# Two cross attentions: a third score bank, maxima inside the query tile, and their transposition a head earlier

## The reference

```python
qh = q.reshape(B, h, dq, Lq)          # q is x: 16 x 128 x 256, h = 8 heads
kh = k.reshape(B, h, dq, Lk)          # k and v are the context
vh = v.reshape(B, h, dv, Lk)
qk = jnp.einsum('bhdq,bhdl->bhql', qh, kh) * scale
sm = jax.nn.softmax(qk, axis=-1)
ret = jnp.einsum('bhql,bhdl->bhdq', sm, vh)
return gamma * ret.reshape(B, Dv, Lq)
```

## Time and profile before

| what | value |
|---|---|
| median of three runs | 1437.89 us (1437.3 to 1447.53) |
| profiled execution | 1438.84 us, its span 1437.1 us |
| busy PE / PEld / DVE / ACT / POOL | 79 / 61 / 64 / 39 / 34% of the span |
| mean granted clock of TensorE | 0.904 of 2.4 GHz |
| DVE's maxima L388, ACT's exponentials L522 | 256 each, 686 and 597 ns |
| PE L296, L316, L318 | 512 each, printed mean 288, 280, 278 ns |

### The profile page before, as it was taken

The page is one execution under the profiler, slowest core; times in us unless marked ns, Lnnn a source line. Parts: engine busy times, 40 slices in busy tenths (PEclk is TensorE's granted clock), DMA queues, the critical chain, the costliest instruction groups (busy, mean ns, idle before and its releaser), DMA issues. The chain is left out here.

```text
span 1437.1 us, 31266 instructions
## 1 busy us (share of the span) xinstructions
PE 1139.4 (79%) x9497; PEld 883.2 (61%) x9568; DVE 915.0 (64%) x2406; ACT 558.5 (39%) x1306; POOL 492.5 (34%) x971
## 2 busy tenths in 40 slices
PE   4599998599964353345999999999999599986997
PEld 4466675366641122125998899898988366654665
DVE  3488995477758999982444444444445378765886
ACT  3245554266642121122323332333233166653553
POOL 5276886233322222221232233223223223322232
PEclk8889999699996667667999999999999699998999
DMA  7899995434424011001010010001001234431111
GB/s 152 176 183 225 189 168 114 115 115 122 128 75 93 23 33 33 25 22 63 12 38 23 29 33 25 22 29 37 22 19 34 83 116 128 124 89 49 55 51 41
DMA packets 145419, 111.84 MB, mean 78 GB/s; under 512 B 17872, under 2 KB 131840, under 8 KB 145344
## 3 DMA queue, kind: packets, MB, share of 16 engines
q1 hardware_dynamic: 132032, 100.01, 28.4%
q10 hardware_dynamic: 11344, 8.72, 2.2%
q0 software_dynamic: 1968, 2.16, 0.9%
HBM read 68.91 MB, written 31.52 MB: 70 GB/s over the span
## 5 line engine op out<-in xcount | busy, mean ns | idle before, releaser
L388 DVE TENSOR_REDUCE ca_nm<-ca_p_s 128x2 f32<-128x512 f32 x256 | 170.5, 686 | 79.4 <-PE ca_p_s L296 72.6
L522 ACT ACTIVATE ca_pt<-ca_p_e 128x512 f32<-128x512 f32 x256 | 152.0, 597 | 89.7 <-PE ca_p_e L318 88.2
L296 PE MATMUL ca_p_s<-ca_ks,ca_qs 96*128 96x256 bf16 x512 | 103.7, 288 | 41.5 <-DMA ca_ks<-k_stack 37.2
L316 PE MATMUL ca_p_e<-ca_qs,ca_ks 96*128 96x256 bf16 x512 | 130.3, 280 | 0.2
L318 PE MATMUL ca_p_e<-ca_mt,row_of 96*128 96x256 bf16 x512 | 129.0, 278 | 0.0
L2064 ACT ACTIVATE la_pq<-la_p_s,la_nm 128x128 f32<-128x128 f32 x256 | 73.2, 369 | 106.2 <-DVE la_nm L2104 106.2
L1897 PE MATMUL la_p_f<-la_qt,q_w 128*128 128x128 f32 x512 | 101.4, 280 | 12.5 <-ACT la_lt L2045 11.3
L1555 PE MATMUL mx_p_i<-identb,mx_qi 128*128 128x128 bf16 x128 | 19.4, 307 | 108.8 <-POOL mx_qi L1406 108.8
L1898 PE MATMUL la_p_f<-la_qt,q_w 128*128 128x128 f32 x512 | 99.0, 275 | 0.0
L296 PEld LDWEIGHTS ca_p_s<-ca_ks,ca_qs 96*128 96x128 bf16 x512 | 45.3, 101 | 69.2 <-DMA ca_ks<-k_stack 30.1
L1897 PEld LDWEIGHTS la_p_f<-la_qt,q_w 128*128 128x128 f32 x512 | 77.6, 192 | 16.3 <-ACT la_lt L2045 16.3
(11 more groups left out here) (282 smaller groups left out, 3009.6 us busy)
## 6 DMA issues: line engine op xcount, KB each, us to landing
sa_qks<-sa_qkp SPq DMA_DIRECT2D x96, 128.0 KB, 4.9
ca_qs<-q_stack SPq DMA_DIRECT2D x64, 192.0 KB, 2.9
ca_ks<-k_stack SPq DMA_DIRECT2D x64, 192.0 KB, 3.2
ca_ct<-in_ctx_t SPq DMA_DIRECT2D x32, 128.0 KB, 3.0
ca_xr<-x_state SPq DMA_DIRECT2D x32, 128.0 KB, 2.1
x_state<-ca_xn SPq DMA_DIRECT2D x32, 128.0 KB, 2.7
k_stack<-sa_cxp SPq DMA_DIRECT2D x16, 192.0 KB, 2.8
q_stack<-sa_parts SPq DMA_DIRECT2D x16, 192.0 KB, 2.6
```

Of the source, the lines that this page charges most:

```text
L296: last = pe.matmul(p_s[h % 2][:, qc, :], QS[u][:, h, 128 * qc:128 * qc + 128], KS[u][:, h, :], start=True, stop=True)
L316: pe.matmul(p_e[h % 2][:, kc, :], KS[u][:, h, 128 * kc:128 * kc + 128], QS[u][:, h, :], start=True, stop=False)
L388: dve.tensor_reduce(NM[u][:, h, :], p_s[h % 2][:, :, :], AX.X, ALU.max, negate=True).then_inc(max_done, 1)
L522: act.activation(PT[h // 4][:, h % 4, :, :], p_e[h % 2][:, :, :], ACT.Exp, scale=SCALE).then_inc(exp_done, 1)
```

## The change

- The maxima's rows go into the query tile itself. QS and KS get 128 partitions: 96 hold the stacks, and 32 more hold the transposed parts of the maxima (QS, written by `copy_max`, four times over, once for each head of the group) and a constant that selects a head's rows (KS, from `picks`). *Shifted* then needs two matmuls of 128 rows instead of four; `MT` goes, and the transposed maxima land on partitions 96 to 127.
- `set_picks` makes `picks` on POOL in the self attention, behind step 13; three copies on DVE put it into the three KS buffers at the start of each cross attention.
- Three banks for scores instead of two: scores of a head wait for the maxima three heads back. `p_r` moves into the bank of `p_t`, and `turn_out` takes over the wait that `turn_back` had.
- QS and KS have three buffers. One load brings all eight heads (384 KB), as soon as the image before the last one has been shifted.
- `turn_max` and `copy_max` stand one head earlier.
- All pairs of images are written out; no loop is left in this stage.

```diff
-        QS = [sb(f"qs{u}", [STACK, H, D], BF16) for u in range(2)]
-        KS = [sb(f"ks{u}", [STACK, H, D], BF16) for u in range(2)]
+        QS = [sb(f"qs{v}", [128, H, D], BF16) for v in range(3)]
+        KS = [sb(f"ks{v}", [128, H, D], BF16) for v in range(3)]
...
-        p_s = [pb(f"p_s{n}", [128, 2, 256], F32) for n in range(2)]
+        p_s = [pb(f"p_s{n}", [128, 2, 256], F32) for n in range(3)]
...
-        p_m = pb("p_m", [96, 4, 256], BF16)
+        p_m = pb("p_m", [128, 4, 256], BF16)
         p_t = pb("p_t", [128, 2, 2, 4, 32], F32)
-        p_r = pb("p_r", [128, 512], F32)
+        p_r = p_t[:, 0].rearrange("p g h c -> p (g h c)")
...
+            def load_stacks(b):
+                wait(sp, shifted_ready, H * (b - 2))
+                load_stack(sp, QS[b % 3], q_stack, b, stack_loaded[b % 3])
+                load_stack(sp, KS[b % 3], sh.k_stack, b, stack_loaded[b % 3])
...
             def pair(i):
                 for u in range(2):
                     b = 2 * i + u
-                    if not is_last(i):
-                        sp.wait_ge(shifted_ready, H * b + 4)
-                        load_half(b + 2, u, 0)
+                    if b + 2 < B:
+                        load_stacks(b + 2)
+                        load_values(b + 2)
                     if follow(i, u):
                         wait(sp, ln_steps, 3 * (b - 1) + 1)
                         sp.dma_start(XR[1 - u][:, :], x_in[b + 1]).then_inc(xr_loaded[1 - u], 16)
-                    if not is_last(i):
-                        sp.wait_ge(shifted_ready, H * b + H)
-                        load_half(b + 2, u, 1)
...
-                wait(pe, max_done, n - 1)
+                wait(pe, max_done, n - 2)
...
                 for kc in range(2):
-                    pe.matmul(p_e[h % 2][:, kc, :], KS[u][:, h, 128 * kc:128 * kc + 128],
-                              QS[u][:, h, :], start=True, stop=False)
-                    last = pe.matmul(p_e[h % 2][:, kc, :], sh.row_of[:, h % 4, :], MT[:, h // 4, :],
-                                     start=False, stop=True)
+                    last = pe.matmul(p_e[h % 2][:, kc, :], KS[(2 * i + u) % 3][:, h, 128 * kc:128 * kc + 128],
+                                     QS[(2 * i + u) % 3][:, h, :], start=True, stop=True)
...
-                wait(pe, norm_steps, 2 * b)
+                wait(pe, ln_steps, 3 * (b - 1) + 1)
...
                     for h in range(H):
-                        if h == 3:
+                        if h == 2:
                             turn_max(i, u, 1)
-                        if h == 7 and later:
+                        if h == 6 and later:
                             turn_max(*later, 0)
...
+            for v in range(3):
+                dve.tensor_copy(KS[v][STACK:128, :, :], sh.picks[STACK:128, :, :]).then_inc(picks_ready, 1)
...
-                n = 2 * (2 * i + u) + g
-                act.wait_ge(mt_ready, n + 1)
-                wait(act, shifted_ready, 4 * (n - 1))
-                act.activation(MT[:, g, :], p_m[:, g, :], ACT.Copy).then_inc(mt_copied, 1)
+
+                b = 2 * i + u
+                act.wait_ge(mt_ready, 2 * b + g + 1)
+                wait(act, shifted_ready, H * (b - 3) + 4 * g + 4)
+                act.activation(QS[b % 3][STACK:128, 4 * g:4 * g + 4, :],
+                               p_m[STACK:128, g:g + 1, :].to_broadcast([128 - STACK, 4, D]), ACT.Copy).then_inc(mt_copied, 1)
...
-                        if h == 2:
+                        if h == 1:
                             copy_max(i, u, 1)
-                        if h == 6 and later:
+                        if h == 5 and later:
                             copy_max(*later, 0)
...
+def set_picks(pool, sh, picks_set):
+
+    rows = sh.picks[STACK:128, :, :]
+    pool.memset(rows, 0.0).then_inc(picks_set, 1)
+    pool.wait_ge(picks_set, 1)
+    for p in range(3):
+        by_group = rows.rearrange("p (g j) c -> p g j c", j=4)
+        pool.affine_select(out=by_group, in_=by_group, compare_op=ALU.not_equal, fill=1.0, base=-4 * p,
+                           pattern=[[0, 2], [-1, 4], [0, D]], channel_multiplier=1).then_inc(picks_set, 1)
+        pool.wait_ge(picks_set, 2 + p)
...
             for b in range(B):
                 step(b)
+                if b == B - 3:
+                    pool.wait_ge(xb_done, b + 1)
+                    set_picks(pool, sh, picks_set)
```

More of the change, by code:

```diff
@@ L93, in __init__ @@
         self.row_of = sb("row_of", [96, 16, 128], BF16)
+        self.picks = sb("picks", [128, 8, D], BF16)
         self.minus_half = sb("minus_half", [128, 1], F32)
@@ L154, with load_stack @@
 STACK_STORES = 3
-def load_stack(eng, tile, stack, b, heads, sem):
-    view = stack[b].rearrange("t (r h) c -> (t r) h c", h=8)
-    eng.dma_start(tile[:, heads, :], view[:, heads, :]).then_inc(sem, 16)
+def load_stack(eng, tile, stack, b, sem):
+    eng.dma_start(tile[0:STACK, :, :], stack[b].rearrange("t (r h) c -> (t r) h c", h=8)).then_inc(sem, 16)
 def cross_attention(nc, sh, name, x_in, q_stack, x_out, ctx_t_in, gamma_in=None):
@@ L272, in pair @@
                         sp.dma_start(XR[1 - u][:, :], x_in[b + 1]).then_inc(xr_loaded[1 - u], 16)
-                    if not is_last(i):
-                        sp.wait_ge(shifted_ready, H * b + H)
-                        load_half(b + 2, u, 1)
-                        sp.wait_ge(values_ready, b + 1)
-                        sp.dma_start(CT[u][:, :, :], ctx_t_in[b + 2].rearrange("(c p) s -> p c s", p=128)).then_inc(ct_loaded[u], 16)
                     if has_older(b):
                         store(b - 2, u)
-            over_pairs(sp, pair)
+            for i in range(PAIRS):
+                pair(i)
             store(B - 2, 0)
@@ L291, in scores @@
                 n = H * (2 * i + u) + h
-                if h % 4 == 0:
-                    pe.wait_ge(stack_loaded[u][h // 4], 32 * (i + 1))
-                wait(pe, max_done, n - 1)
+                b = 2 * i + u
+                if h == 0:
+                    pe.wait_ge(stack_loaded[b % 3], 32 * (b // 3 + 1))
+                wait(pe, max_done, n - 2)
                 for qc in range(2):
-                    last = pe.matmul(p_s[h % 2][:, qc, :], QS[u][:, h, 128 * qc:128 * qc + 128],
-                                     KS[u][:, h, :], start=True, stop=True)
+                    last = pe.matmul(p_s[n % 3][:, qc, :], QS[b % 3][0:STACK, h, 128 * qc:128 * qc + 128],
+                                     KS[b % 3][0:STACK, h, :], start=True, stop=True)
                 last.then_inc(scores_ready, 1)
@@ L343, in turn_back @@
                 pe.wait_ge(norm_steps, 2 * b + 2)
-                wait(pe, ln_steps, 3 * (b - 1) + 1)
                 for qc in range(2):
@@ L374, in pair @@
                             turn_back(b - 1)
-            over_pairs(pe, pair)
+            for i in range(PAIRS):
+                pair(i)
             weigh(B - 1, 1, 1)
@@ L446, in pair @@
                                 residual(b - 1, 1 - u, pi)
-            over_pairs(dve, pair)
+            for i in range(PAIRS):
+                pair(i)
             normalise(B - 2, 0, PAIRS - 1)
@@ L474, in parts @@
                 rest = NR[:, :, :]
-                part = [MP[:, g, :, 32 * p:32 * p + 4] for p in range(3)]
+                part = [MP[:, g, :, STACK + 4 * p:STACK + 4 * p + 4] for p in range(3)]
                 pool_copy(pool, sh, part[0], new).then_inc(part_steps, 1)
@@ L504, in pair @@
                         rstd(b - 1)
-            over_pairs(pool, pair)
+            for i in range(PAIRS):
+                pair(i)
             rstd(B - 1)
@@ L539, in pair @@
                             copy_out(b - 1)
-                        if h == 2:
+                        if h == 1:
                             copy_max(i, u, 1)
-                        if h == 6 and later:
+                        if h == 5 and later:
                             copy_max(*later, 0)
-            over_pairs(act, pair)
+            for i in range(PAIRS):
+                pair(i)
             copy_out(B - 1)
```

27 lines of the change are left out of this document (14 added, 13 removed).

## The result

| | before | after |
|---|---|---|
| median of 15 executions | 1441.81 us (1433.36 to 1447.53) | 1432.67 us (1428.12 to 1437.82) |
| profiled execution, span | 1438.84, 1437.1 us | 1432.41, 1430.1 us |
| one image of the steady stretch ("walk"), first and second cross attention | 9.42, 9.28 us | 8.59, 8.59 us |
| first stage, first DMA of SP to last `turn_back` | 161.5 us | 152.3 us |
| second stage, the same | 159.4 us | 150.9 us |

The ratio is 0.9938, 95% interval 0.992 to 0.9955: about 9 us faster (6.5 to 11.5), where 22.6 were forecast. That is "no change" by the prediction's bound of 1%.

A forecast was written before the change was run, and what follows sets the result against it. TensorE was taken to lead, with VectorE not far behind; afterwards ScalarE and TensorE in turn. Terms -31.0 - 1.0 + 4.2 + 5.2 = -22.6 us gave 1416.2 from 1438.84, forecast 1416, range 1394 to 1436 for 8 in 10.

The forecast's parts named there:

- the walk of 8.3 us: Cross attentions: one steady image followed through ScalarE and TensorE, 8.3 us against 9.42 and 9.28, -31.0 us in all.
- the new copy holds ScalarE 0.92 us: Copy of maxima, 32 x 1024: 1.02 us less 0.10 overlap with the next instruction, twice an image.
- The ring: Named after measuring: ScalarE's copy, exponential, TensorE's two heads, `weigh`, then output copy or transposition; halves of 4.50 and 4.08 us.
- The two bubbles: ScalarE idle behind `weigh` in each image: 0.8 us before the output copy, 0.9 before the next maxima copy.
- The last image: End of each cross attention: without scores, half a microsecond less a stage, -1.0 us in all.
- `set_picks`: Self attention: GpSimd's memset and selects stall TensorE 4.2 us, then the lower clock costs 1.0; +5.2 together.
- The starts: Start of each cross attention: larger first load +1.5 us, longer first copy +0.6; twice, +4.2.
- B (parts late): GpSimd's parts of the maxima use up the slack: 9.1 us an image, 1440 us, no change; chance 0.20.
- A: Bubbles close and VectorE's work plus small waits bind: 7.3 us an image, 1387 us; chance 0.12.
- C: Less busy TensorE drops to 1.2 GHz: 4.8 us more per affected image, 1464 us with ten; chance 0.06.
- D: Stacks still load late behind the residual's input in SP's queue: 8.8 us an image, 1431 us; chance 0.04.
- the forecast case of 8.0 to 8.8: Main case: 8.0 to 8.8 us an image, 1405 to 1432 us, starts and `set_picks` within bounds; chance 0.58.

The follow-up runs named there:

- copy_short: Changed kernel, but from the fourth image ScalarE copies the turned maxima for one head of each group of four; 1416.63 us, ratio 0.9826, walk 8.00 us.
- paired_spread: Changed kernel with selects spread as in picks_spread and the maxima's copy moving bf16 pairs as four-byte words; 1405.83 us, ratio 0.9751.
- paired_normalise: paired_spread with VectorE's normalisation behind the maxima of head 1 in place of head 0; 1401.24 us, ratio 0.9729, walk 7.73 us.
- picks_spread: Changed kernel with the three selects of picks one each behind the splits of images 13, 14 and 15; 1423.69 us, ratio 0.9886.
- turn_first: Changed kernel with maxima transposed ahead of `weigh` and copied ahead of the output copy; 1434.83 us, ratio 0.9949, walk 8.73 us.
- own_turn_late: Changed kernel with four matmuls a head, short copy, no picks, maxima turned at heads 3 and 7; three banks stay; 1420.97 us, ratio 0.9845.

## Why the prediction was wrong

Sign and mechanism held, the size did not: -9 us for -22.6. The time is inside the range of 1394 to 1436, near its upper end.

**The step that failed is the walk of 8.3 us**, in its terms "the new copy holds ScalarE 0.92 us" and the output copy at 0.50. In the timeline above they are 1.04 and 0.62. Both took off an overlap of 0.10 with the next instruction, read in the earlier trace rows from an exponential with the old copy behind it and from the old copy with an exponential behind it. On neither side of the new copy is there any: 1.02 printed and 1.04 to the next start, 0.60 printed and 0.62 from output copy to copy. The ring holds two copies and an output copy: 2 x 0.12 + 0.12 = 0.36 us, of which other links gave 0.1 back. The exponentials at 0.53 did no harm: those whose scores are ready start 0.494 apart. In each four the third starts 0.66 behind the second, since it waits 0.07 for TensorE's shift, which makes 0.547 on average. The rest is that the text rounded 8.33 to 8.3. So -31.0 became (9.42 - 8.59 + 9.28 - 8.59) x 14.75 = **-22.4**, 8.6 us less. The two bubbles stood where the walk put them, 0.61 for 0.8 and 0.8 for 0.9, both released by TensorE. That the copy's length sets the walk is shown by copy_short and paired_spread, down to VectorE's bound of 8.00, and by paired_normalise below it.

The Trainium skill ("ScalarE: Activation LUTs", What ACT_TABLE_LOAD costs) gives an ACTIVATE with immediate operands 186 ns and 0.833 ns an element, fp32 and bf16 alike, and says that instructions back to back overlap by about 93 ns. The three sizes agree with the first (0.399, 0.613, 1.039 by the page; 0.376, 0.591, 1.016 measured), and by the slope pairing the bf16 takes nearly half off the copy. The second held between exponentials that were ready (0.597 printed, 0.494 apart) and behind the old copy of 96 partitions (0.38 printed, 0.28 to the next start), and not around the copy of 32 partitions.

**The last image** was forecast 0.5 us shorter a stage and is 0.38 longer: its two steps are 7.76 and 4.87 us for 7.21 and 5.04. Without scores the first step of the two is 2.2 us shorter than the walk where TensorE's work sets it, 0.83 where the ring does. Two stages: **+0.8** for -1.0.

**`set_picks`** was forecast at +5.2 and cost **+6.9** (picks_spread). The stall of 4.07 was right to 0.1; the low clock behind it lasted 5.4 us and cost 2.4, inside the bounds of 0 and 3 but not the 1.0 I took. The rest of its price, 0.4, has no place, and it is less than the spread between traces.

**The starts** were forecast at +4.2 and cost +5.1 to the first shift: 12.77 for 9.76 us in the first stage, 11.31 for 9.21 in the second. From there to the first `turn_back` are 1.75 images; in both stages together they are 1.3 us faster than the difference of the walks gives, which leaves **+3.8**. The three copies of picks took 2.73 us together, under the lower bound of 3.6, and stayed hidden.

-22.4 + 0.8 + 3.8 + 6.9 = **-10.9**, inside the measured 6.5 to 11.5. It is no proof of itself: the +3.8 is what the two stages, 9.3 and 8.5 us shorter, leave over. The profiled pair shows -7.0 with its 3.6 us of drift. Of the 11.7 us between this sum and -22.6 the walk is 8.6, the last images 1.8, `set_picks` 1.7, and the starts give 0.4 back.

**The rivals.** B (parts late) did not happen: the parts were 0.9 and 1.35 us early. turn_first shows what that slack hangs on: with the transposition ahead of `weigh` TensorE waits 0.7 and 0.8 us for them. A (7.3 us with VectorE the bound) had the next bound right in kind, wrong in size: VectorE holds at 8.00, and 7.73 was the best reached. C: the clock stayed full in the steady images. D: no stack was waited for. The walk of 8.59 lies in the forecast case of 8.0 to 8.8, and the median of 1432.67 just above its 1405 to 1432. The chance of 0.58 for a gain over 1% hung on an edge at 8.55 us an image with 8.33 forecast, and an error of 0.06 us in each of four links crosses that edge.

One thing the prediction's own numbers said and I did not draw: it counted 8.3 us of TensorE's work an image before, and 8.3 us for the walk after. A kernel that only lost its waits would have been as fast. own_turn_late, which keeps all of TensorE's work and has no wait for a bank, is nearly that kernel: 8.35, and 1420.97 us.

## What to carry to other kernels

Before moving work from the full engine to an idle one, price what removing its waits alone gives; a third score bank was worth 0.75 to 0.85 us an image with TensorE's work left as it was, and the moved work, once it lay in a ring, made a walk 0.24 us longer than that. When no engine is full and two wait for each other, write the ring link by link from starts (not printed durations): what counts is only what lies on it, here the copy, cut to 0.58 of its time by moving pairs of bf16 as one word. One-time work behind which a full engine waits costs its length, less the slack, and the slow clock after; cut in pieces behind the last short jobs it cost 1.3 us at most.

## What was not expected of the hardware

- A ScalarE copy of 32 partitions takes 0.376, 0.591 and 1.016 us for 256 and 512 and 1024 elements: as 512 words of four bytes the same bytes are copied in 0.58 of the time.
- ScalarE's exponentials overlap by 0.10 us where their scores are ready (0.597 printed, 0.494 apart), and so did the old copy of 96 partitions with the exponential behind it (0.38 printed, 0.28 to the next start). The copy of 32 partitions overlaps with nothing, at any of its three lengths: whatever is on either side of it, the next start is 0.024 us behind the end. Whether it is the number of partitions, their place from 96 on or something else in the form, no run separates.
- A pause of 3.07 us on TensorE was followed by 5.4 us at 1.2 GHz; the steady walk with pauses of 0.9 and 0.7 us in each image kept 2.4 GHz.
- At the first stage's start 768 KB of stacks were there 5.9 us after the second issue (273.62 to 279.54), for 3.3 us with 384 KB; in the second stage 4.9 (1134.64 to 1139.56) for 2.8. Forecast was 4.8 for 3.3. One issue of SP among the first stage's loads took 2.06 us, for 0.4 of the others, and 1.6 to 2.0 in the other twelve kernels.
